# Expert gates broadcast by DMA and applied on GpSimd, four PSUM banks for values, in a two-stage attention and expert kernel

## What is computed

```python
t = _to_tokens(x)
t = t + _L1_attn_ref(_ln_t(t), L1_attn_W_kv, L1_attn_q_proj)
t = t + _L1_ffn_ref(_ln_t(t), L1_ffn_router_w, L1_ffn_router_b, L1_ffn_expert_w, L1_ffn_expert_b)
```

```python
top_p, top_i = jax.lax.top_k(router_probs, K)
top_p = top_p / jnp.sum(top_p, axis=-1, keepdims=True)
```

## Time and profile before

| | us |
|---|---|
| median of 3 runs | 2888.69 |
| lowest and highest | 2887.95, 2891.39 |
| the profiled execution's own time | 2888.39 |
| its span, first to last instruction | 2886.6 |
| busy: TensorE matrix multiplications | 2684.3 (93%) |
| busy: VectorE | 2257.9 (78%) |
| busy: ScalarE | 1860.3 (64%) |
| busy: GpSimd | 1759.8 (61%) |
| mean granted TensorE clock | 0.976 |

### The profile page before, as it was taken

How to read it: one execution, slowest core, us unless ns; L and a number is a source line. 1 busy time by engine, 2 the same in 40 slices (tenths; PEclk the granted TensorE clock), 3 DMA queues, 4 the chain that set the end, 5 groups by cost and what they waited for, 6 DMA issues and landing times. The chain is left out here.

```text
span 2886.6 us, 37812 instructions
## 1 busy us (share of the span) xinstructions
PE 2684.3 (93%) x11363; PEld 1942.6 (67%) x11363; DVE 2257.9 (78%) x3469; ACT 1860.3 (64%) x3400; POOL 1759.8 (61%) x1441
## 2 busy tenths in 40 slices
PE   5999999999999999999999999968789998998888
PEld 3788877788887788886788888734445555555443
DVE  5788777788887788787778878525888898898996
ACT  3666677666676667667766666747766665665540
POOL 1677767777776777776777777824544444443430
PEclk8999999999999999999999999989999999999889
DMA  1000000000000000000000000033323323323220
GB/s 62 1 8 4 5 8 5 34 4 8 5 5 4 5 37 5 5 8 5 4 5 8 4 5 8 4 96 140 125 99 132 114 79 145 104 83 129 89 77 26
DMA packets 39165, 122.35 MB, mean 42 GB/s; under 512 B 6352, under 2 KB 8976, under 8 KB 29744
## 3 DMA queue, kind: packets, MB, share of 16 engines
q1 hardware_dynamic: 38960, 119.93, 11.8%
HBM read 102.55 MB, written 17.37 MB: 42 GB/s over the span
## 5 line engine op out<-in xcount | busy, mean ns | idle before, releaser
L174 POOL TENSOR_TENSOR p_lo<-pf,p_hi 128x512 fp32r<-128x512 f32 x1024 | 1322.9, 1295 | 452.3 <-ACT p_hi L403 449.4
L398 ACT ACTIVATE pf<-s_ps 128x512 f32<-128x512 f32 x1024 | 613.7, 599 | 542.2 <-PE s_ps L273 540.7
L501 DVE TENSOR_REDUCE mx<-m_ps 128x1 f32<-128x512 f32 x1024 | 703.1, 688 | 325.6 <-PE m_ps L254 318.6
L517 DVE TENSOR_TENSOR sum_ps<-sum_ps,pf 128x512 f32<-128x512 f32 x960 | 661.7, 689 | 23.6 <-ACT pf L398 23.3
L403 ACT CAST p_hi<-pf 128x512 fp32r<-128x512 f32 x1024 | 629.1, 614 | 0.0
L271 PE MATMUL s_ps<-q_hi,kd_hi 128*128 128x512 f32 x1024 | 427.6, 418 | 0.0
L886 POOL TENSOR_TENSOR acc<-acc,ay 128x512 f32<-128x512 f32 x192 | 255.7, 1332 | 281.7 <-DVE ay L1223 281.2
L254 PE MATMUL m_ps<-kp,q_hi 128*128 128x512 f32 x1024 | 405.6, 398 | 20.6 <-DVE mx L501 19.8
L285 PE MATMUL om_ps<-p_hi,v_hi 128*128 128x512 f32 x1024 | 400.9, 392 | 4.6 <-POOL p_lo L174 4.6
L272 PE MATMUL s_ps<-q_hi,kd_lo 128*128 128x512 f32 x1024 | 399.7, 390 | 0.0
L273 PE MATMUL s_ps<-q_lo,kd_hi 128*128 128x512 f32 x1024 | 399.7, 390 | 0.0
(11 more groups left out here) (213 smaller groups left out, 3680.8 us busy)
## 6 DMA issues: line engine op xcount, KB each, us to landing
bq<-weight_rows SPq DMA_DIRECT2D x64, 1024.0 KB, 4.9
xb<-in_x_dram SPq DMA_DIRECT2D x8, 1024.0 KB, 6.1
tokens<-xb SPq DMA_DIRECT2D x32, 256.0 KB, 2.0
tp<-tokens SPq DMA_DIRECT2D x32, 256.0 KB, 5.3
rb<-norm_rows SPq DMA_DIRECT2D x32, 256.0 KB, 4.2
tv<-tokens SPq DMA_DIRECT2D x32, 256.0 KB, 5.4
out_dram<-tv SPq DMA_DIRECT2D x32, 256.0 KB, 2.4
bq<-in_L_attn_W_kv_dram SPq DMA_DIRECT2D x1, 1024.0 KB, 8.2
```

What stands on the lines that cost most here:

```text
L174: nc.gpsimd.tensor_tensor(p_lo[:, r, :], pf[:, r, :], p_hi[:, r, :].bitcast(F32), ALU.subtract).then_inc(lo_done, 1)
L398: nc.scalar.activation(pf[:, g % RING, :], s_ps[:, g % 2, :], ACT.Exp, scale=SCALE).then_inc(exp_done, 1)
L501: nc.vector.tensor_reduce(mx[:, n % 2, sub, chunk:chunk + 1], m_ps[:, j % 2, :], AX.X, ALU.max).then_inc(m_max, 1)
L517: nc.vector.tensor_tensor(sum_ps[:], sum_ps[:], p, ALU.add).then_inc(sum_done, 1)
```

## The change

- The gates no longer go to all partitions through TensorE (`spread`) and PSUM. ScalarE copies the turned gates from PSUM to `l_sb` as well, SyncE writes them to a DRAM tensor `gate_rows` (four small DMAs a super block), and for each block reads them back broadcast to 128 partitions into `gb`, in two halves of 1 MB, each as soon as its half of `gb` has been used.
- The product of gate and token block, `gated`, moves from VectorE to GpSimd. It stands first in each slot of GpSimd's queue, before `scaled`, `low` and `add_head`. `xg` has two buffers in place of three.
- The two banks of `g_ps` go to the values: `v_ps` has four, and `value(v, h)` waits for the scan of slot h-4.
- The gates are computed one slot earlier, ScalarE's tanh moves from slot 4 to 2, and `turn_gates` and `hold_gates` from slot 7 to 5.

```diff
+            def gate_rows(s):
+                sp.wait_ge(gr_act, s + 1)
+                for b in range(B):
+                    sp.dma_start(gates_d[s, b, :, :], l_sb[QUAD * b:QUAD * b + E, :]).then_inc(gr_out, 16)
+
+            def gate_spread(i, j):
+                s, b, cols = place(i)
+                sp.wait_ge(gr_out, 16 * B * (s + 1))
+                if i:
+                    sp.wait_ge(xg_pool, (i - 1) * E + HALF * (j + 1))
+                sp.dma_start(gb[:, j, :, :].rearrange("p e n -> p (e n)"),
+                             gates_d[s, b:b + 1, HALF * j:HALF * (j + 1), :].rearrange("o e n -> o (e n)")
+                             .to_broadcast([C, HALF * TOK])).then_inc(gb_in[j], 16)
...
                 if stage(v + 1):
                     weight_spread(v + 1, 1)
+                if stage(f + 1):
+                    if (f + 1) % B == 0:
+                        gate_rows((f + 1) // B)
+                    gate_spread(f + 1, 0)
+                    gate_spread(f + 1, 1)
...
+            def gated(f, e):
+                pool.wait_ge(gb_in[e // HALF], 16 * (f + 1))
+                after(pool, x_pe, f * E + e - 1)
+                if e == 0:
+                    pool.wait_ge(t2_dve, f + 1)
+                nc.gpsimd.tensor_tensor(xg[:, e % 2, :], gb[:, e // HALF, e % HALF, :], tv[:, f % NV, :],
+                                        ALU.mult).then_inc(xg_pool, 1)
+
             scaled(0)
             low(0)
             for j in range(STEPS):
-                k, v = j, j - V_LAG
+                k, v, f = j, j - V_LAG, j - F_LAG
                 for h in range(HEADS):
+                    if stage(f):
+                        gated(f, h)
                     if stage(k + 1) and h == 1:
                         scaled(k + 1)
...
-                after(pe, y_dve, v * HEADS + h - 1)
-                project(v_ps[:, h % 2, :], h, 1, v).then_inc(v_pe, 1)
+                after(pe, y_dve, v * HEADS + h - 3)
+                project(v_ps[:, h % 4, :], h, 1, v).then_inc(v_pe, 1)
...
-            def spread(f, e):
...
             def expert(f, e):
-                pe.wait_ge(xg_dve, f * E + e + 1)
-                pe.matmul(mo_ps[:], ew[:, e, :], xg[:, e % 3, :], start=False, stop=(e == E - 1)).then_inc(x_pe, 1)
+                pe.wait_ge(xg_pool, f * E + e + 1)
+                pe.matmul(mo_ps[:], ew[:, e, :], xg[:, e % 2, :], start=False, stop=(e == E - 1)).then_inc(x_pe, 1)
...
-                    if norm2_at(j, 2) is not None and h == 7:
+                    if norm2_at(j, 2) is not None and h == 5:
                         turn_gates(norm2_at(j, 2))
...
             def hold_gates(s):
                 act.wait_ge(gt_pe, s + 1)
+                act.wait_ge(lt_pe, s + 1)
+                nc.scalar.copy(l_sb[:], st_ps[:]).then_inc(gr_act, 1)
                 nc.scalar.copy(gt[:, s % 2, :], st_ps[:]).then_inc(gt_act, 1)
...
-            def gated(f, e):
-                dve.wait_ge(g_pe, f * E + e + 1)
-                after(dve, x_pe, f * E + e - 2)
-                nc.vector.tensor_tensor(xg[:, e % 3, :], g_ps[:, e % 2, :], tv[:, f % NV, :], ALU.mult).then_inc(xg_dve, 1)
...
```

More of the change, by code:

```diff
@@ L640, in scan_attention_and_experts @@
     rows_d = nc.dram_tensor("weight_rows", (SUPERS, B * 2, HALF, TOK), F32, kind="Internal").ap()
+    gates_d = nc.dram_tensor("gate_rows", (SUPERS, B, E, TOK), F32, kind="Internal").ap()
     rs_d = nc.dram_tensor("norm_rows", (SUPERS, B, TOK), F32, kind="Internal").ap()
@@ L662, in scan_attention_and_experts @@
         ident, center = sb("ident1", [C, C]), sb("center", [C, C])
-        sel = sb("sel", [C, B, E], F32R)
         late = sb("late", [C, E])
@@ L679, in scan_attention_and_experts @@
         carry = sb("carry", [C, B, HEADS])
-        xg = sb("xg", [C, 3, TOK])
+        xg = sb("xg", [C, 2, TOK])
+        gb = sb("gate_b", [C, 2, HALF, TOK])
         m_r, e_r, u_r, b_r = (sb(n, [C, TOK]) for n in ("m_r", "e_r", "u_r", "b_r"))
@@ L692, in scan_attention_and_experts @@
         ewf = bq[:, 1, 0:2, :].rearrange("p h n -> p (h n)")
-        v_ps = psum("v_ps", [C, 2, BANK])
+        v_ps = psum("v_ps", [C, 4, BANK])
         k_ps = psum("k_ps", [C, BANK])
         row_ps = psum("row_ps", [C, BANK])
-        g_ps = psum("g_ps", [C, 2, BANK])
         mo_ps = psum("mo_ps", [C, BANK])
@@ L720, in scan_attention_and_experts @@
             sem(n) for n in ("var2_dve", "msq2_act", "ln2_act", "rst2_act", "gate", "th_act"))
-        gt_pe, gt_act, g_pe, xg_dve, x_pe, out_dve = (
-            sem(n) for n in ("gt_pe", "gt_act", "g_pe", "xg_dve", "x_pe", "out_dve"))
+        gt_pe, gt_act, gr_act, gr_out, xg_pool, x_pe, out_dve = (
+            sem(n) for n in ("gt_pe", "gt_act", "gr_act", "gr_out", "xg_pool", "x_pe", "out_dve"))
+        gb_in = [sem(f"gb_in{i}") for i in range(2)]
+        clr = sem("clr")
         block = ctx.enter_context(nc.Block())
@@ L863, in _ @@
             nc.gpsimd.memset(eb_lo[:].bitcast(F32), 0.0).then_inc(cst2, 1)
+            nc.gpsimd.memset(g32[:], 0.0).then_inc(clr, 1)
             def scaled(i):
@@ L985, in expert_bias @@
                 after(pe, out_dve, f)
+                pe.wait_ge(gt_act, s + 1)
                 pe.matmul(mo_ps[:], eb_hi[:, b, :], gt[:, s % 2, :], start=True, stop=False)
@@ L998, in _ @@
             for g in range(HALF):
-                dst = v_ps if g < 2 else g_ps
                 for i in range(TT):
-                    mm = pe.transpose(dst[:, g % 2, i * C:(i + 1) * C], wkv[:, g * TT + i, :], ident[:])
+                    mm = pe.transpose(v_ps[:, g, i * C:(i + 1) * C], wkv[:, g * TT + i, :], ident[:])
                 mm.then_inc(wt_pe, 1)
@@ L1011, in _ @@
             pe.wait_ge(ec_act, 3)
-            pe.wait_ge(cst3, 6)
+            pe.wait_ge(cst3, 5)
             for j in range(STEPS):
@@ L1016, in _ @@
                 for h in range(HEADS):
-                    if stage(f) and h == 0:
-                        spread(f, 0)
                     if stage(v):
                         value(v, h)
-                    if stage(f) and h + 1 < E:
-                        spread(f, h + 1)
                     if stage(k - 1) and h == 0:
@@ L1075, in silu_value @@
                 act.wait_ge(v_pe, v * HEADS + h + 1)
-                nc.scalar.activation(v_ps[:, h % 2, :], v_ps[:, h % 2, :], ACT.Silu).then_inc(v_act, 1)
+                nc.scalar.activation(v_ps[:, h % 4, :], v_ps[:, h % 4, :], ACT.Silu).then_inc(v_act, 1)
             def old_weight(v, h):
@@ L1091, in hold_logits @@
                 act.wait_ge(lg_pe, s + 1)
+                after(act, gr_out, 16 * B * s)
                 nc.scalar.copy(l_sb[:], st_ps[:]).then_inc(lg_act, 1)
@@ L1117, in _ @@
                 act.wait_ge(wt_pe, g + 1)
-                src = v_ps if g < 2 else g_ps
                 nc.scalar.copy(w_hi[:].rearrange("p h w c -> p (h w c)")[:, g * BANK:(g + 1) * BANK],
-                               src[:, g % 2, :]).then_inc(wt_hi, 1)
+                               v_ps[:, g, :]).then_inc(wt_hi, 1)
                 if g == 1:
@@ L1166, in _ @@
                         high(k + 1)
-                    if norm2_at(j, 2) is not None and h == 4:
+                    if norm2_at(j, 2) is not None and h == 2:
                         s = norm2_at(j, 2)
@@ L1213, in weigh @@
                 dve.wait_ge(v_act, v * HEADS + h + 1)
-                zv = v_ps[:, h % 2, :]
+                zv = v_ps[:, h % 4, :]
                 nc.vector.tensor_tensor(zv, bq[:, q % 3, h % HALF, :], zv, ALU.mult).then_inc(z_dve, 1)
@@ L1222, in scan @@
                     dve.wait_ge(y_pool, (v - B) * YP + (HALF if h < HALF else YP))
-                nc.vector.tensor_tensor_scan(ay[:, h, :], ay[:, h, :], v_ps[:, h % 2, :],
+                nc.vector.tensor_tensor_scan(ay[:, h, :], ay[:, h, :], v_ps[:, h % 4, :],
                                              0.0 if s == 0 else carry[:, b, h:h + 1], ALU.mult, ALU.add).then_inc(y_dve, 1)
@@ L1278, in gates @@
                                             ALU.add).then_inc(gate, 1)
-                if slot == 1:
+                if slot == 0:
                     ready(3)
                     first_of(lg, top1, place1, pick1, 3)
-                if slot == 2:
+                if slot == 1:
                     ready(8)
@@ L1287, in gates @@
                     first_of(lg, top2, place2, pick2, 9)
-                if slot == 3:
+                if slot == 2:
                     nc.vector.tensor_tensor(gap[:], top1[:], top2[:], ALU.subtract).then_inc(gate, 1)
@@ L1291, in gates @@
                     nc.vector.tensor_tensor(work, pick1[:], pick2[:], ALU.subtract).then_inc(gate, 1)
-                if slot == 5:
+                if slot == 3:
+                    dve.wait_ge(clr, 1)
                     dve.wait_ge(th_act, s + 1)
@@ L1299, in gates @@
                     ready(19)
-                    nc.vector.tensor_tensor(x[:, :, 0:E], x[:, :, E:2 * E], wide(rst2), ALU.mult).then_inc(gate, 1)
-                if slot == 6:
```

(13 more changed lines are left out.)

## The result

The changed kernel takes 3051.65 us, median of 4 runs (3046.54 to 3058.67), against 2888.32 for the kernel before on the same chip: a ratio of 1.0568, 95% interval 1.0542 to 1.0593. It is slower, as forecast, by 163 us where I had said 117. 3051.65 lies inside the range of 2915 to 3080.

A forecast was written before the change was run, and what follows sets the result against it. It took TensorE to bound plain steps before, and a ring of waits over two slots after. 70 (steps 11 to 31), 10 (clock), 32 (steps 32 to 36) and 5 (end) on 2888.4 gave 3005 us, range 2915 to 3080.

The forecast's parts named there:

- The ring: Closed loop of waits through TensorE, ScalarE, VectorE and GpSimd queues: 7.15 us per two slots, about 28.3 a step.
- The rival "faster": Ring does not bind, GpSimd's rate of 22.3 us a step does: 2826 us in total; chance 0.05.
- The rival "longer stalls": Same ring, clock low half the time, DMA wait at upper end, gates' round trip uncovered: 3069 us; chance 0.20.
- A plain step: Step with j % 4 = 3, values and experts without extras: about 28.3 us from the ring, against 23.6 before.
- Steps with j % 4 = 2: First choices on VectorE, two copies on ScalarE, the turn on TensorE: 1.5 us on top of 28.3.
- Steps with j % 4 = 0 and 1: Extras on 28.3: reciprocal and table changes 2.0; ScalarE's slot 7 and TensorE's statistics 3.3, DMA wait 4.2.
- The DMA wait: Steps with j % 4 = 1: first gate half queued behind the new weights' broadcast, mean wait 4.2 us.
- Steps 32 to 36: Steps without keys, partly at the lower clock: 162 us against 129.7, so +32.
- The banks at nothing: Two more value banks only relax a wait; counted at 0, up to 6 us possible in steps 5 to 10.
- The end: Steps 39 to 42 unchanged; step 38's last gates also take the trip through DRAM: +5 us.
- The sum: Whole kernel: 70 + 10 + 32 + 5 = 117 us on top of 2888.4, giving 3005.
- the clock's term: TensorE's lower clock in full steps: one fall a group of four steps, 2 us each, +10 in all.

The follow-up runs named there:

- e1: Changed kernel with gated(f, h+1) put before add_head(v, h) in GpSimd's queue, one slot ahead: 2916.91 us, ratio 1.0097 to the kernel before.
- e8: Changed kernel with expert(f, h) put behind value(v, h+1) in TensorE's queue, GpSimd's order left alone: 2921.86 us, ratio 1.0110 to the kernel before.
- e9: e3 with two unused multiplications added on TensorE ahead of each expert's wait, only in slots 1 to 4, 6 and 7: 3047.66 us.
- e10: Changed kernel with gated a slot ahead, first gate half before new weights, last six steps' products on VectorE, expert behind next value: 2838.35 us.
- e4: Changed kernel with SyncE issuing the first gate half before it waits for the new weights, in steps with j % 4 = 0: 3031.93 us.
- e3: Changed kernel with values back in two of the four banks, waiting for the scan of slot h-2: 3051.87 us.
- e2: Changed kernel with the product gated moved back from GpSimd to VectorE, gates still coming by DMA: 2942.81 us, ratio 1.0183 to the kernel before.
- e7: e3 with two unused multiplications added on TensorE ahead of each expert's wait, in every slot with an expert: 3057.65 us.

## Why the prediction was right, point by point

- **The ring**: right. The turn was forecast at 7.15 us and is 7.21; GpSimd's product at 1.29 and is 1.287. e1 and e8 open it from two sides and get back 135 and 130 us. Its links give a plain step's length at best: 28.3 forecast, 29.5 without a fall of the clock (e9).
- **The rival "faster"**, GpSimd's rate without a ring: its rate was about right (22.3 us a step forecast, plain steps of 22.6 in e10, where TensorE is nearly as full), and the condition it was given, a ring shorter than two of today's slots, did not hold.
- **The rival "longer stalls"**, 3069: the measured time is nearer to it (17 us) than to my 3005 (47 us), but its terms are not what happened. The clock was low for 89 of 663 us in steps 12 to 31, not half of them. The first product waited 3.2 to 4.8 us for its gates, in steps with j % 4 = 1 alone, not the 7.8 of its upper end. No product of steps 12 to 31 waited for the gates' trip through DRAM.
- **A plain step**: 28.3 forecast, 30.4 measured, mis-sized by 2.1. By e9's plain steps about 0.9 of it is the clock: at least one fall a step, where I had one in four steps (before the change the clock was low for 21 us of these 20 steps). The rest is in the first four slots: slot 0 has the row sums and the biases on TensorE, so that its expert starts 2.19 us after its product (2371.65 to 2373.84 in step 19) and not 1.32; slot 1 has `residual` ahead of the next weighing (0.26 us), and GpSimd's addition beside it takes 1.63 us in place of 1.29 (2378.38). I had let the slack of a slot swallow most of this. As I read it, the two chains of the ring run through one queue, and a late one holds the other; no run tries that alone.
- **Steps with j % 4 = 2**: 1.5 us of extras forecast, 4.0 above the plain step measured. Of the extras this term was mis-sized most. The timeline of step 22:

```profile
2473.63 0.60 ACT L1096 ACTIVATE v_ps<-v_ps 128x512 f32<-128x512 f32 x1
...
2474.66 0.27 DVE L1292 TENSOR_TENSOR st_ps<-st_ps,rst 128x128 f32<-128x128 f32 x1
...
2476.62 0.29 DVE L1288 TENSOR_TENSOR pick<-st_ps,place 128x128 f32<-128x128 f32 x1
2476.82 0.69 DVE L1237 TENSOR_TENSOR v_ps<-bq,v_ps 128x512 f32<-128x512 f32 x1
```

The silu of slot 1 starts at 2473.63; the weighing would follow at 0.68, but VectorE's choice of the first expert stands ahead of it (L1292 to L1288, seven small operations one behind the other), and it starts 3.19 us later. In slot 2 the second choice does the same (2478.00 to 2481.17). So both chains are held by 2.5 us, one after the other; I had counted only what goes beyond VectorE's slack in a slot.
- **Steps with j % 4 = 0 and 1**: 30.3 and 35.8 forecast (28.3 with 2.0, and with 3.3 and 4.2), 32.5 and 35.4 measured. Above the plain step of each they are 2.1 and 5.0 against 2.0 and 7.5. The DMA wait of 4.2 was worth 3.3 (e4), so the 3.3 for ScalarE and TensorE was worth some 1.7. In the forecast of that wait 2.65 and 1.2 us stood without a row; together they had the product wanted 8.6 us after the new weights, and GpSimd was free for it after 9.2.
- **Steps 32 to 36**: 162 forecast, 167.4 measured. Clock 0.82 there, against 0.86.
- **The banks at nothing**: right for the total (e3). In the first steps with values they do give a little, of the up to 6 us that the forecast allowed. The first 32 scans start within 73.6 us in the changed kernel and 76.0 in e3; over all traces it is 71.6 to 74.0 with four banks and 76.0 to 77.0 with two:

```profile
L1245 DVE TENSOR_TENSOR_SCAN ay<-ay,v_ps x32: 1219/1221/1222, 1978.4 to 2052.0; 128x512 f32<-128x512 f32 x32
...
L1245 DVE TENSOR_TENSOR_SCAN ay<-ay,v_ps x32: 1219/1220/1222, 1981.0 to 2057.0; 128x512 f32<-128x512 f32 x32
```

- **The end**: +5 forecast. Steps 38 to 42 took 64.3 us against 55.6, +8.7, and step 37 4.6 more. The stretches are steps 37, 38, 39 and 40 to 42:

```profile
2967.30:2984.50 17.20, 14.01 (x38) 4.44 (x38) 2.48 (x6) 4.63 (x8) 13.13 (x11) 0.80 0.32 116
2984.50:2995.90 11.40, 9.45 (x22) 3.34 (x22) 7.30 (x23) 1.29 (x3) 8.75 (x7) 1.00 0.33 110
2995.90:3014.40 18.50, 11.42 (x18) 3.42 (x18) 0.69 (x2) 0.00 (x0) 11.33 (x9) 0.82 0.54 191
3014.40:3048.80 34.40, 27.60 (x54) 8.51 (x54) 2.07 (x4) 0.00 (x0) 28.70 (x24) 1.00 0.48 172
```

The gates' trip shows in step 39: from the first store at 2994.30 to the first product at 3001.45 it is 7.15 us, against the 7.1 of the earlier trace rows, and that product had waited 6.81 us for it. Since step 38 is shorter than before, 11.4 us against 14.1, the two steps together cost 4.6 us more, and here the +5 was right. The other 4.1 us are in steps 40 to 42, forecast at nothing. They take 11.4 each, not GpSimd's 10.3: with two buffers `xg` the third product waits for the first expert, and that for `output` of the block before, 1.1 us a block (GpSimd's idle time at 3028.22 and 3039.59 us). That wait I had not followed. In step 37 GpSimd waits 3.8 us for experts, with TensorE's clock at 0.80; what its 4.6 us come from stays open.
- **The sum**: by stretch the 165.5 us between the two spans are 5.4 up to step 12, 109.1 in steps 12 to 31, 37.7 in steps 32 to 36, 4.6 in step 37 and 8.7 after. Forecast, with step 11 counted at 3: 3, 77, 32, 0 and 5. In steps 12 to 31 the plain length was 2.1 us short in all 20 steps, 42 us, of which the clock's term had 10. The extras of j % 4 = 2 were 12.5 us short in five steps, and those of j % 4 = 1 12.5 us too long, so that these two errors cancel by chance. The mechanism was right, and the term most in error is the length of a full step.

## What to carry to other kernels

When an operation moves to another queue, write down what stands before it and behind it in each queue and close the loops: a loop's links from the trace, summed, over the number of slots that it spans, is the best rate, however idle the engines are. Moving it one slot ahead in its new queue cost nothing here and was worth 135 us. And with the loop open, look for what it had covered: the broadcast behind the weights went from 4.4 us of idle time to 7.6.

## What was not expected of the hardware

- VectorE's product of two SBUF tensors took 953 ns in the mean beside GpSimd and 689 alone (e2); with one input in PSUM 681 beside it. The gates in PSUM had spared VectorE this.
- A fall of TensorE's clock in this ring is worth 0.7 to 0.9 us in a plain step by e9, 0.3 to 0.5 by e7, and could not be seen in the total: e9 halved the time at the lower clock in steps 12 to 31, from 82 to 44 us, and stood within its interval of e3.
